# A decoder layer on one core: first stretch reordered with a shorter norm chain, second half's first norm moved in among the first sixty units

## The reference

```python
x = x + attention(layernorm(x), w_qkv, b_qkv, w_o, b_o)
    # 32 query heads, 8 key/value heads of 32; rotary embedding on q and k; causal softmax; output projection
x = x + matmul(fake_quant(layernorm(x)), fake_quant(ctx))   # ctx: 2 x 1024 x 1024, 0..255 levels
h = layernorm(x)
x = x + h @ W_org.T + sum over 8 experts of coeff_e * (h @ down_e @ up_e)
    # coeff = softmax over experts of keys @ Wq @ mean over tokens of h
layernorm(x) = (x - mean) / sqrt(var + 1e-5)
```

## Time and profile before

| | |
|---|---|
| time, median of runs | 731.07 us |
| the profiled execution: time / span of its instructions | 732.93 / 731.1 us |
| TensorE busy | 669.8 us, 92% |
| VectorE, ScalarE busy | 428.2 us (59%), 424.2 us (58%) |
| GpSimd busy | 298.9 us (41%) |
| mean granted TensorE clock | 0.958 |

### The profile page before, as it was taken

One profiled execution on the slowest core, in us unless ns is written; L12 is line 12 of the kernel. 1 busy time (PEld: TensorE's weight loads), 2 busy tenths in 40 slices (PEclk: granted clock), 3 DMA queues, 4 the chain that ended last, 5 costly groups with the idle time before them and its releaser, 6 DMA issues.

```text
span 731.1 us, 12781 instructions
## 1 busy us (share of the span) xinstructions
PE 669.8 (92%) x4512; PEld 537.4 (73%) x4512; DVE 428.2 (59%) x1147; ACT 424.2 (58%) x1025; POOL 298.9 (41%) x360
## 2 busy tenths in 40 slices
PE   3889699999999999999889699999999698999998
PEld 3888477888777777878656477787877576788886
DVE  5677467776777734665776965443236788821112
ACT  4335377877878746779967675656215682611320
POOL 2057744544433363357320650505715014814520
PEclk9889799999999989999998889999999989999999
DMA  6606855554445524423562340404326253423102
GB/s 236 245 25 200 247 179 160 171 169 110 131 145 166 152 106 113 129 56 91 174 200 93 83 125 18 140 5 123 140 85 230 70 185 105 155 76 116 43 15 100
DMA packets 43822, 93.47 MB, mean 128 GB/s; under 512 B 5488, under 2 KB 5872, under 8 KB 42224
## 3 DMA queue, kind: packets, MB, share of 16 engines
q1 hardware_dynamic: 34416, 66.45, 28.1%
q0 software_dynamic: 3584, 15.73, 8.9%
q10 hardware_dynamic: 5760, 10.49, 3.9%
HBM read 72.72 MB, written 19.92 MB: 127 GB/s over the span
## 4 chain that ended last, share of the span: by engine, by line
PE 67%; DVE 13%; ACT 7%; issue 5%; POOL 4%; DMA 3%; ACTq 0%; DVEq 0%
PE dense L1029 44%; PE probt L921 8%; PE score L909 5%; PE pv L936 5%; DVE stats L1322 2%; ACT prob_all L1123 1%; POOL w_lo L1590 1%; DMA q_stack<-rope_dram 1%; PE misc L945 1%; DVE w_lo L1258 1%; PE misc L975 1%; ACT stage L1072 1%; DMA stage<-in_ctx_kv 1%; DVE xres L1394 1%; DVE ln_s L832 1%
## 5 line engine op out<-in xcount | busy, mean ns | idle before, releaser
L1029 PE MATMUL dense<-w_hi,act_t 128*128 128x512 f32 (+1 forms) x684 | 230.3, 397 | 7.3 <-DVE act_t L1341 2.7
L1278 DVE CUSTOM_DVE_ANT_0 prob_all<-score,mask_sb 128x128 f32<-128x128 f32 (+3 forms) x256 | 123.4, 488 | 125.2 <-PE score L909 123.3
L1590 POOL TENSOR_TENSOR w_lo<-stage,w_hi 128x512 fp32r<-128x512 f32 x85 | 110.7, 1311 | 195.1 <-ACT w_hi L1076 194.8
L1123 ACT ACTIVATE prob_all<-prob_all,neg_max 128x128 f32<-128x128 f32 (+3 forms) x256 | 142.7, 558 | 41.3 <-DVE neg_max L1278 40.1
L1029 PEld LDWEIGHTS dense<-w_hi,act_t 128*128 128x128 f32 x684 | 131.4, 198 | 32.1 <-POOL w_lo L1590 4.5
L1029 PE MATMUL dense<-act_t,w_hi 128*128 128x512 f32 x408 | 139.2, 423 | 2.7 <-DVE w_lo L1258 1.3
L1029 PE MATMUL dense<-w_lo,act_t 128*128 128x512 f32 (+1 forms) x372 | 137.4, 390 | 1.0 <-ACT w_lo L1081 0.8
L921 PE MATMUL probt<-ident_sb,prob_all 128*128 128x128 f32 x640 | 114.6, 279 | 3.7 <-ACT prob_all L1132 3.1
L909 PE MATMUL score<-k_stack,q_stack 96*128 96x128 f32 (+3 forms) x256 | 91.1, 360 | 9.5 <-DMA q_stack<-rope_dram 7.1
L1132 ACT ACTIVATE prob_all<-probt 128x128 f32<-128x128 f32 (+3 forms) x160 | 68.7, 430 | 50.0 <-PE probt L921 49.4
L1076 ACT ACTIVATE w_hi<-stage 128x512 fp32r<-128x512 f32 x117 | 71.7, 622 | 43.8 <-PE dense L1029 31.2
(11 more groups left out here) (156 smaller groups left out, 875.6 us busy)
## 6 DMA issues: line engine op xcount, KB each, us to landing
q_stack<-rope_dram POOLq DMA_DIRECT2D x16, 768.0 KB, 7.7
stage<-in_w_qk SPq DMA_DIRECT2D x40, 256.0 KB, 2.8
rope_dram<-act_t ACTq DMA_DIRECT2D x40, 256.0 KB, 2.5
stage<-in_w_o SPq DMA_DIRECT2D x32, 256.0 KB, 2.9
stage<-in_ctx_kv SPq DMA_DIRECT2D x24, 256.0 KB, 3.5
stage<-in_w_org SPq DMA_DIRECT2D x24, 256.0 KB, 3.1
xres<-in_x SPq DMA_DIRECT2D x8, 512.0 KB, 6.5
prob_all<-in_x SPq DMA_DIRECT2D x8, 512.0 KB, 7.0
```

The lines of the kernel that those rows point to most:

```text
L1029: last = engine.matmul(dst, lhs, rhs, start=(k == 0 and c == 0), stop=(k == g.kts - 1 and c == len(pairs) - 1))
L1123: engine.activation(prob[:, u % P_SLOTS, 0:length], prob[:, u % P_SLOTS, 0:length], ACT.Exp, bias=neg_max[:, m:m + 1], scale=-1.0, accum_o ...
L1278: engine.tensor_tensor_reduce(prob[:, u % P_SLOTS, 0:length], score_bank[u % 2][:, 0:length], mask_sb[:, S - length:S], -1.0, HIGHEST, ALU ...
L1590: engine.tensor_tensor(slot_lo(p, 0, NW), raw_of(p), slot_hi(p, 0, NW).bitcast(F32), ALU.subtract).then_inc(g_piece, 1)
```

## The change

1. `norm_scale` is another chain: the variance is scaled, a guess from the bits, one Newton link with other constants, and a second step written as a polynomial of the residue, with the last two operations of the quantised norm folded into one. On VectorE and GpSimd alike it is 8 operations where it was 10 (10 in place of 13 for the quantised norm, two of them beside others).
2. The first stretch is eight slots in place of four (v0 | v1 | k0 | k1 on tokens 0 to 255 | v2 | v3 | k0 | k1 on 256 to 511). Tile 1's transposes come in the middle of v0, tile 2's before k1, tile 3's in the middle of v2. x is loaded earlier among the weight pieces. The chains of the first half are written apart from the statistics.
3. The second half's tiles no longer have `x_second`. Each is loaded into one of the two `xnorm` buffers (tile t + 2 after the transposes of tile t), and load, statistics, chain, normalisation, transposes (in `misc_bank`) and copies get slots from the planner: loads at 12 and 3 slots before the first unit and at units 9 and 15, transposes at units 5, 8, 12, 14, 22, 24, 28, 31.
4. GpSimd's program puts `add_sine` and `rope_low` ahead of the weight low parts. The first group's keys and queries have a load of their own as early as they can be issued, the queries in two halves of two heads.

```diff
+HEAD = 8
+SECOND_AT = 20
+LOAD_US = 6.0
@@ Plan.__init__
-        for t in range(NT):
-            self.add_tile(v, t)
-            for g in ks if t % 2 else []:
-                self.add_tile(g, t // 2)
-            self.token_ends.append(len(self.steps))
+        for g, n in [(v, 0), (v, 1), (ks[0], 0), (ks[1], 0), (v, 2), (v, 3), (ks[0], 1), (ks[1], 1)]:
+            self.add_tile(g, n)
+            self.head_ends.append(len(self.steps))
@@ due_norms
+        if j == HEAD + SECOND_AT:
+            self.norms += [{"no": (1, 1, t), "from": 1 << 30} for t in range(NT)]
...
+            if which == 1 and "load" not in norm:
+                if x >= 2 and not self.past(j, ("turn", 1, 1, t - 2, 1), 1):
+                    break
+                self.note("load", j, t)
+                norm["load"] = now
+            if which == 1 and now >= norm["load"] + LOAD_US:
+                norm["from"] = min(norm["from"], j)
@@ sync_program
             def load_second(t):
-                engine.dma_start(x_second[:, t, :], x[1, t * P:(t + 1) * P, :]).then_inc(d_xb[t], 16)
+                if t >= 2:
+                    e.wait_ge(t_xt, turned_no(1, 1, t - 2, 1) + 1)
+                engine.dma_start(xnorm[:, t % 2, :], x[1, t * P:(t + 1) * P, :]).then_inc(d_xb[t], 16)
@@ norm_scale
-            ln(engine.tensor_scalar(ve, var, EPS, None, ALU.add))
-            ln(engine.tensor_scalar(vh, var, EPS, -0.5, ALU.add, ALU.mult))
+            ln(engine.tensor_scalar(w, var, EPS, -ROOT_SCALE, ALU.add, ALU.mult))
             wait_ln()
-            ln(engine.tensor_scalar(guess, ve.bitcast(I32), -0.5, RSQRT_SEED, ALU.mult, ALU.add))
-            for link in range(3):
-                g = y if link else guess.bitcast(F32)
-                wait_ln()
-                ln(engine.tensor_scalar(tmp, g, g, vh, ALU.mult, ALU.mult))
-                wait_ln()
-                ln(engine.tensor_scalar(y, tmp, 1.5, g, ALU.add, ALU.mult))
+            ln(engine.tensor_scalar(guess, w.bitcast(I32), -0.5, RSQRT_SEED, ALU.mult, ALU.add))
+            if which == 2:
+                ln(engine.tensor_scalar(mean, mean, -1.0, None, ALU.mult))
+            wait_ln()
+            ln(engine.tensor_scalar(tmp, guess.bitcast(F32), guess.bitcast(F32), w, ALU.mult, ALU.mult))
+            wait_ln()
+            ln(engine.tensor_scalar(root, tmp, NEWTON, guess.bitcast(F32), ALU.add, ALU.mult))
+            wait_ln()
+            ln(engine.tensor_scalar(tmp, root, root, w, ALU.mult, ALU.mult))
+            wait_ln()
+            ln(engine.tensor_scalar(tmp, tmp, SERIES[0], tmp, ALU.add, ALU.mult))
+            if which == 2:
+                ln(engine.tensor_scalar(root, root, inv_scale[:, 0:1], None, ALU.mult))
+            wait_ln()
+            ln(engine.tensor_scalar(y, tmp, SERIES[1], root, ALU.add, ALU.mult))
             wait_ln()
...
-            ln(engine.tensor_tensor(y, y, inv_scale[:, 0:1], ALU.mult))
-            wait_ln()
-            ln(engine.tensor_scalar(tmp, mean, y, -1.0, ALU.mult, ALU.mult))
-            wait_ln()
-            return engine.tensor_tensor(shift_by, tmp, quant_sb[:, 1:2], ALU.add)
+            return engine.tensor_scalar(shift_by, mean, y, quant_sb[:, 1:2], ALU.mult, ALU.add)
@@ tensor_program
                 for s in range(first, end):
-                    if j == 1 and s == first + 2 * KD:
+                    if (j, s) in ((0, first + KD // 2), (3, first), (4, first + KD // 2)):
                         for half in range(2):
-                            turn_tokens(1, 0, j + 1, half)
+                            turn_tokens(1, 0, j - 1 if j else 1, half)
@@ score
-                e.wait_ge(d_qstack[gi % 2], 16 * (gi // 2 + 1))
+                if gi:
+                    e.wait_ge(d_qstack[gi % 2], 16 * (gi // 2 + gi % 2))
+                else:
+                    e.wait_ge(d_qfirst[h // 2], 16)
@@ gpsimd_program
+                for m in rope_add_at.get(j, ()):
+                    add_sine(m)
+                for m in rope_low_at.get(j, ()):
+                    rope_low(m)
                 for p in at["low"].get(j, ()):
...
-                for m in rope_add_at.get(j, ()):
-                    add_sine(m)
-                for m in rope_low_at.get(j, ()):
-                    rope_low(m)
+                if j == first_queries_at:
+                    load_first_keys()
+                    for pair in range(GROUP // 2):
+                        load_first_queries(pair)
```

154 lines of the change are left out of this document (82 added, 72 removed).

## The result

The changed kernel takes 721.02 us (median of 4 runs, 720.63 to 721.42) against 731.37 for the kernel before (4 runs, 728.11 to 732.81): a ratio of 0.9865, interval 0.9831 to 0.9898. The forecast was 711, range 704.5 to 720. The sign is right, and half of the gain is missing. The profiled execution took 721.42, its span is 719.6, so the spans differ by 11.5 where the sum had 19.9. (The profiled execution before lay 1.6 above its median, this one 0.4 above, so the medians differ by 10.4.)

What follows compares the result with a forecast made beforehand. TensorE, busy 92% of the span, was taken as the bound, its prologue ending with a query load hung on GpSimd's order. -22.2 + 0.9 - 1.5 + 2.8 + 3 - 2.9 = -19.9 gave 711 us, range 704.5 to 720.

Steps and rivals of the forecast that it cites:

- The first projections: Start of the kernel: key projections end at 40.8 us, 8.4 before 49.2; query projections then end at 64.8 against 80.5.
- The first query load: Path to the first score: issue near 59.2, 6.2 us to land, first score 65.4 against 87.6, so -22.2.
- The bound of -19.9: Worst case of the first-score term of -22.2; said to hold two VectorE/GpSimd port meetings costing 2 us.
- +0.9: Units 0 to 2: delays from the query load's second half and tile 0's statistics before the first maximum (0 to +2).
- -1.5: Clock after the first score: half of the half-clock stretch vanishes with a gap of 0.6 us (0 to -3.1).
- +2.8: Units: 32 transposes of the second half come in, 8 x 0.35 us, since TensorE is full there.
- +3: Units: stalls from the second half's normalisation and statistics on ScalarE and VectorE, 1 + 1 + 0.5 + 0.5 (0 to +9).
- The late chains: Second half's output projection and two later VectorE chains: shorter norm chain saves 2.1 + 0.8, together -2.9 us (-1 to -4).
- C: Rival: query load takes 12 us or GpSimd's path meets VectorE at every step; first score near 72, 717.8; chance 0.07.
- B: Rival: ScalarE and VectorE bound the first two groups of 16 units, +9 not +3, low clock stays; 718.7; chance 0.18.
- signs of being wrong: First score after 70 or before 64; first score to end over 10 us longer (643.5 before); first-projection wait over 2 us.

Runs made afterwards that it cites:

- a_fastq: Changed kernel with the first query tile's rotation ahead of two VectorE low parts of weights, and its addition, low part, store and loads earlier: 721.15 us, ratio 0.9877.
- a_oldchain: Changed kernel with the norm chain of before (three links; 10 operations, 13 for the quantised norm), nothing else: 724.78 us, 0.9904 of the kernel before.
- a_late3: Changed kernel with the statistics of the second half's tile 3 at units 24 and 25 in place of 20 and 21, later steps following: 719.43 us, ratio 0.9818.
- a_best5: Changed kernel with earlier first-query path and x loads, additions before chains, tile 0's chain on VectorE, later tile 3 statistics and third/fourth query tile steps: 711.96 us, ratio 0.9731.

## Why the prediction was wrong

**The first projections, right.** Key projections end at 41.0 (40.8 forecast), query projections at 64.8 (64.8). The gain there, 15.7 us on 80.5, is as worked out.

**The first query load, the first step that failed.** "First score 65.4 against 87.6: -22.2" was -16.5. The issue came at 62.9, not 59.2, and the load took 8.1, not 6.2. In the other three profiles of the same program up to there, the issue is at 62.5 to 62.6 and the load takes 6.6 to 7.5, so the late issue is the steady part. Of its 3.7 us, 3.0 stand in one place, VectorE in front of the rotation (47.69 to 51.18; the rotation was forecast for 48.2):

```profile
47.69 3.49 DVE L1270 TENSOR_TENSOR w_lo<-stage,w_hi 128x512 fp32r<-128x512 f32 x2
51.21 2.28 DVE L1410 SCALAR_TENSOR_TENSOR xres<-dense,bias_qk,rope_sb 64x512 f32<-64x512 f32 x3
53.41 0.68 DVE L1270 TENSOR_TENSOR w_lo<-stage,w_hi 128x512 fp32r<-128x512 f32 x1
```

```profile
62.87 1.05 POOL L1606 DMA_DIRECT2D q_stack<-rope_dram  x2 [0.68 <-DMA rope_dram<-xres]
```

I had counted GpSimd's two low parts of weights and not VectorE's two, though the order of VectorE's program shows them. a_fastq, with one of the two behind the rotation, moved the issue to 59.9 and so shows this. Their number is the smaller part of it. The same operation takes 0.68 us at 53.41, while GpSimd does nothing, and these two took 3.49, each beside an operation of GpSimd (46.40 to 48.94 and 49.28 to 50.63): about 2.1 of the 3.0 us are these meetings, which the prediction put at 2 and laid inside a bound. The 6.2 was a mean between "half the bytes" and "beside traffic"; the halves took what the whole took, and the whole 8.1. The bound of -19.9 is the longest load of the rows, 8.5, behind the issue as forecast, 59.2, and left no room for a late issue: a bound on one factor was taken for a bound on the term.

**Units 0 to 32, the second step that failed.** +0.9, -1.5, +2.8 and +3 make +5.2; it was +11.0. Leaving the norm out shows 8.0 of it to be that work, and its timeline puts the other 3.0 to the exponentials behind GpSimd's additions. The same 11.0 by kind:

- Stalls, +4.4, near the +3.9 of the two terms, but by luck: there was no wait for the load's second half (+0.9), since the first half came so late itself. 3.0 are waits for a low part on VectorE that frees the bank of the transposes, where waits for a maximum or a normalised tile were forecast, and 1.7 are waits for exponentials.
- The clock, about +2.4 in place of -1.5 (by the windows 0.11 of 49.7 against 0.08 of 38.7 us). The -1.5 rested on a gap of 0.6 us before the first score; it was 6.3, and the half clock lasted until 79. A second stretch at half clock, 110 to 113, came behind the wait of 2.12.
- The transposes, what is left, 11.0 - 4.4 - 2.4 = 4.2: 0.5 for each of the eight groups where 0.35 was taken. A second set cost 0.44, and the group that starts at 92.79, with the next score at 93.20, shows 0.41. At full clock from score 8 to 16 the two groups there cost 0.70 each ((11.37 - 9.58 - 0.39) / 2); what they cost beyond 0.41 lies in the products around them and is not taken apart further.

And there is a step that the prediction did not have, an overlap put at nothing. It moved the units 16 us forward against GpSimd's queue, and "Behind each new wait stand the maximum or the exponential" looked at the norm's own waits alone, not at the additions of the third and fourth query tile, which ScalarE waits for with the exponentials behind it. The norm chain in front of the third tile's addition makes that wait longer (6.60 us in the changed kernel, 3.71 without the norm) but isn't its cause.

**The late chains, right.** -2.9 forecast; -2.9 behind score 254 (234.7 to 231.8), and a_oldchain gives it back (235.1). From the aggregate to the operation behind the chain it took 2.97 (567.44 to 570.41) and takes 2.36 (a chain of the same kind, another tile's):

```profile
567.41 0.22 DVE mean_var L1340
...
569.77 0.69 DVE xnorm L1366
```

GpSimd's later chains were put at 0, and a_oldchain bears that out. The 3.1 us between score 32 and 254 were not forecast. 1.1 of them lie in score 128 to 144, which takes 26.8 us before and 25.7 after, at a clock of 0.87 and 0.93; a_fastq has 24.1 at 1.00 and a_late3 26.9 at 0.87 there, with edits that lie far ahead of that stretch, so this part is no effect of the change. Another 1.5 lie in score 176 to 192 (37.4 to 35.9), where the shorter chain alone gives 36.1. The kernel before has one profile, so more can't be said.

**The rivals.** The size of C ("first score near 72") came true with 71.1, and nearly that of B, which has 12.7 for the units where 11.0 was measured. Their causes did so in part: the load took 8.1 and not 12, and GpSimd's path met VectorE; the clock stayed low, but ScalarE and VectorE are busy for 37.9 and 36.6 of the 49.7 us, so it is the order in their queues and not their load that makes the waits. I had priced B and C as alternatives, 0.18 and 0.07, each on top of a forecast that was right elsewhere. They are not alternatives; together they give 725, outside a range that had been built from one at a time. Of the signs of being wrong, the first score after 70 came; the time from it to the end is 648.5, 5.0 longer than before and not 10, and the first projections hold no long wait. That a_best5 takes 711.96 doesn't bear the 711 out: it has other edits than the change that was forecast.

## What to carry to other kernels

When a stage is moved, walk every engine's queue at the new place, and for each waiting instruction ask what stands behind it, and what stands behind that on the engine it releases: here VectorE's low parts before a rotation, and GpSimd's additions before ScalarE's exponentials. Waits in series hide each other, so an edit that gains nothing alone is no proof that its wait is harmless; remove the next one too. And when two risks have different causes, price them together.

## What was not expected of the hardware

Two loads of 384 KB issued 0.5 us apart landed after 8.1 and 8.5 us, a load of 768 KB at the same place after 8.1. The first half's load took 4.2 to 9.3 us over the runs, and 6.6 and 9.3 in two executions of one program up to it. A low part of weights on VectorE took 0.68 us while GpSimd was idle and about 1.8 beside an operation of GpSimd. The granted clock fell after a wait of 2.12 us of TensorE, about 1.5 us after the work had resumed (0.50 from 110 to 113). Behind waits of 2.05 to 2.13 us at that place it fell in six of nine profiles, behind 1.3 to 1.7 us in none of five; but in a_best5 it fell at 76.6 behind a wait of 1.20. So the length of the last wait does not settle it.
